# A batched transformer chain on one core: TensorE runs identity products into a bank before some of its waits, in the first three and last two batches

## The reference

```python
x = x + attn_a(layernorm(x), ...)   # latent attention: 16 heads, causal softmax over 512 keys
x = x + ffn(layernorm(x), ...)      # mixes each token with the one before it, then
x = x + attn_b(layernorm(x), ...)   #   sigmoid(xr @ W_r) * (relu(xk @ W_k)**2 @ W_v)
x = x + ffn(layernorm(x), ...)      # attn_b: queries and keys normalised per head, scale 8
```

## Time and profile before

| what | value |
|---|---|
| median of 3 runs | 1092.72 us (1090.68 to 1095.87) |
| profiled execution, its own time | 1093.79 us |
| its span, first to last instruction | 1092.0 us |
| mean granted TensorE clock | 0.951 |
| PE busy | 946.0 us (87%) |
| DVE busy | 877.3 us (80%) |
| ACT busy | 768.5 us (70%) |
| POOL busy | 281.8 us (26%) |

### The profile page before, as it was taken

The page is one execution under the profiler, slowest core; times in us unless marked ns, Lnnn a source line. Parts: engine busy times, 40 slices in busy tenths (PEclk is TensorE's granted clock), DMA queues, the critical chain, the costliest instruction groups (busy, mean ns, idle before and its releaser), DMA issues.

```text
span 1092.0 us, 37313 instructions
## 1 busy us (share of the span) xinstructions
PE 946.0 (87%) x15889; PEld 516.0 (47%) x15889; DVE 877.3 (80%) x2112; ACT 768.5 (70%) x1042; POOL 281.8 (26%) x264
## 2 busy tenths in 40 slices
PE   4687978888989899999999999998989899899694
PEld 1333444444544445454555545454545455455352
DVE  3977767889788898989899898989898888864633
ACT  2165557677767778787777778887777778788581
POOL 6111213223133131322223132223223232222212
PEclk8598889899999999999999999999999999999797
DMA  5243413455417062442617162543628170405220
GB/s 148 76 97 99 119 45 85 118 127 129 128 57 189 22 190 57 138 119 84 172 48 198 36 186 54 144 106 104 152 69 186 41 195 22 119 3 127 72 57 20
DMA packets 94342, 112.95 MB, mean 103 GB/s; under 512 B 15200, under 2 KB 81888, under 8 KB 94176
## 3 DMA queue, kind: packets, MB, share of 16 engines
q1 hardware_dynamic: 94176, 110.56, 38.6%
HBM read 55.22 MB, written 54.53 MB: 100 GB/s over the span
## 4 chain that ended last, share of the span: by engine, by line
PE 44%; DVE 31%; ACT 15%; issue 6%; POOL 1%; DMA 1%; SPq 0%; DVEq 0%; POOLq 0%; ACTq 0%
PE acc L729 14%; DVE rowmax L1081 11%; ACT prob L930 10%; PE pool L712 6%; PE pool L595 4%; PE pool L643 4%; PE pool L762 3%; DVE xn L1039 3%; PE pool L784 3%; PE pool L609 3%; DVE stats L1027 2%; PE pool L770 2%; PE pool L659 2%; DVE rest_k L1052 2%; PE pool L681 2%
## 5 line engine op out<-in xcount | busy, mean ns | idle before, releaser
L930 ACT ACTIVATE prob<-pool 128x1024 f32<-128x1024 f32 x576 | 565.3, 1030 | 136.3 <-PE pool L659 132.8
L1081 DVE TENSOR_REDUCE rowmax<-pool 128x2 f32<-128x1024 f32 (+7 forms) x480 | 357.2, 791 | 64.9 <-PE pool L659 62.2
L729 PE MATMUL acc<-prob,vals_a 128*32 128x512 f32 (+7 forms) x2048 | 167.7, 422 | 0.2 <-ACT prob L930 0.2
L729 PE MATMUL acc<-prob,vals_b 128*32 128x512 f32 (+7 forms) x2048 | 162.8, 418 | 1.5 <-DVE turned_b L1117 1.1
L643 PE MATMUL pool<-stack_ka,stack_qa 48*64 48x512 bf16 (+7 forms) x2048 | 117.0, 301 | 39.7 <-ACT prob L930 12.7
L712 PE MATMUL pool<-stack_qa,stack_ka 51*64 51x512 bf16 (+7 forms) x2048 | 113.3, 301 | 32.6 <-DVE rowmax L1081 18.4
L659 PE MATMUL pool<-mask_t,ident_b 64*64 64x128 bf16 (+1 forms) x2304 | 129.5, 215 | 0.0
L712 PE MATMUL pool<-stack_qb,stack_kb 48*64 48x512 bf16 (+7 forms) x2048 | 112.4, 295 | 17.1 <-ACT prob L930 8.3
L643 PEld LDWEIGHTS pool<-stack_ka,stack_qa 48*64 48x64 bf16 x2048 | 42.8, 108 | 131.8 <-issue 46.8
L1292 POOL TENSOR_TENSOR rstd<-mv,minus_half 128x4 f32<-128x4 f32 x64 | 65.4, 1022 | 146.1 <-DVE mv L1034 146.1
L712 PEld LDWEIGHTS pool<-stack_qa,stack_ka 51*64 51x64 bf16 x2048 | 42.8, 108 | 88.2 <-issue 26.3
(11 more groups left out here) (129 smaller groups left out, 1380.5 us busy)
## 6 DMA issues: line engine op xcount, KB each, us to landing
stack_qa<-scratch_qa SPq DMA_DIRECT2D x64, 192.0 KB, 4.9
stack_ka<-scratch_ka SPq DMA_DIRECT2D x64, 192.0 KB, 4.9
stack_kb<-scratch_kb SPq DMA_DIRECT2D x64, 192.0 KB, 3.9
stack_qb<-scratch_qb SPq DMA_DIRECT2D x64, 192.0 KB, 4.8
scratch_qa<-parts_q SPq DMA_DIRECT2D x16, 384.0 KB, 2.8
scratch_ka<-parts_k SPq DMA_DIRECT2D x16, 384.0 KB, 4.8
scratch_qb<-parts_q SPq DMA_DIRECT2D x16, 384.0 KB, 2.6
scratch_kb<-parts_k SPq DMA_DIRECT2D x16, 384.0 KB, 2.9
```

Of the source, the lines that this page charges most:

```text
L729: last = eng.matmul(acc[32 * j:32 * j + 32, BLK * blk:T], vals[a][:, blk, GROUP * g + j, :], prob[n % NPROB][:, k, at:at + T - BLK * blk], ...
L930: eng.activation(prob[n % NPROB][:, :, :], place["unit", n][0][:, :, :], ACT.Exp, scale=scale).then_inc(S["exped"], 1)
L1081: last = eng.tensor_reduce(to, of, axis=AX.X, op=ALU.max)
```

## The change

A row `"warm"` is added to each plan: one number for each of 22 places, named in `WARM_AT`. A new function `warm` issues so many products of the float32 identity with itself, 128 x 128 by 128 x 128, into the bank that the next product will overwrite. It is called between the wait for the bank and the wait for the input. No other number of the plans is changed, and no other engine's instructions are. A number counts once for each occurrence of its place in a batch (`max rows`, for one, occurs twice).

```diff
+WARM_AT = ("max", "max rows", "unit", "xnT1", "qa", "ka", "valsa", "ya", "xnT2", "k2", "r2", "v2", "xnT3", "qk", "qb", "kb",
+           "valsb", "wo", "xnT4", "k4", "r4", "v4")
...
     0: {
+        "warm": [0, 1, 0, 0, 0, 0, 5, 0, 1, 0, 0, 1, 3, 0, 0, 0, 2, 0, 0, 0, 0, 3],
...
     1: {
+        "warm": [0, 2, 0, 6, 1, 0, 0, 0, 0, 0, 0, 0, 0, 0, 0, 0, 0, 0, 2, 0, 0, 2],
...
     2: {
+        "warm": [0, 0, 0, 0, 0, 0, 0, 0, 0, 0, 0, 1, 0, 0, 0, 0, 0, 0, 1, 0, 0, 0],
...
     -2: {
+        "warm": [0, 0, 0, 0, 2, 2, 3, 0, 0, 0, 0, 0, 0, 0, 0, 0, 0, 0, 0, 0, 0, 0],
...
     -1: {
+        "warm": [0, 0, 0, 3, 0, 0, 0, 0, 0, 4, 0, 1, 5, 0, 0, 0, 0, 7, 4, 6, 2, 0],
...
+            def warm(self, ps, at, b):
+
+                plan = PLANS.get(b, PLANS.get(b - B, PLANS[None]))
+                for _ in range(plan["warm"][WARM_AT.index(at)]):
+                    self.eng.matmul(ps[:, 0:P], ident[:, :], ident[:, :], start=True, stop=True)
...
                 ps, freed = place["xnT" + n, b]
                 q.wait_free(freed)
+                self.warm(ps, "xnT" + n, b)
                 q.wait_ge(S["xn" + n], b + 1)
```

More of the change, by code:

```diff
@@ L35 @@
     None: {
+        "warm": [0, 0, 0, 0, 0, 0, 0, 0, 0, 0, 0, 0, 0, 0, 0, 0, 0, 0, 0, 0, 0, 0],
         "load": [-137],
@@ L617, in project @@
                     q.wait_free(freed)
+                    self.warm(ps, n + "a", b)
                     q.wait_ge(S["xnT1"], b + 1)
@@ L634, in row_maxima @@
                     q.wait_free(freed)
+                    self.warm(ps[:, 0, :], "max", b)
                     pieces = sum(max_pieces(*unit, NB), [])
@@ L666, in max_rows @@
                 q.wait_free(freed)
+                self.warm(ps, "max rows", b)
                 q.wait_ge(S["mpart2"], 2 * b + g + 1)
@@ L677, in values @@
                 q.wait_free(freed)
+                self.warm(ps, "vals" + a, b)
                 q.wait_ge(S["xnT" + n], b + 1)
@@ L699, in attend @@
                         q.wait_free(freed)
+                        self.warm(ps[:, 0, :], "unit", b)
                         q.wait_ge(S[f"stacked_q{a}{g}"], 32 * (b + 1))
@@ L739, in normalise @@
                     q.wait_free(freed)
+                    self.warm(ps, "ya", b)
                     q.wait_ge(S["outT_a"], GROUPS * b + g + 1)
@@ L754, in feed_forward @@
                 q.wait_free(freed)
+                self.warm(ps, "k" + n, b)
                 q.wait_ge(S["xk" + n], b + 1)
@@ L759, in feed_forward @@
                 q.wait_free(freed)
+                self.warm(ps, "r" + n, b)
                 q.wait_ge(S["xr" + n], b + 1)
@@ L767, in feed_forward @@
                 q.wait_free(freed)
+                self.warm(ps, "v" + n, b)
                 q.wait_ge(S["act" + n], b + 1)
@@ L780, in project_qk @@
                     q.wait_free(freed)
+                    self.warm(ps, "qk", b)
                     q.wait_ge(S["xnT3"], b + 1)
@@ L799, in turn_qk @@
                     q.wait_free(freed)
+                    self.warm(ps, n + "b", b)
                     q.wait_ge(S["qk"], 2 * (b + 1))
@@ L810, in output_sum @@
                 q.wait_free(freed)
+                self.warm(ps, "wo", b)
                 q.wait_ge(S["yT"], b + 1)
```

## The result

| | before | with the change |
|---|---|---|
| median | 1094.0 us (8 runs, 1090.68 to 1095.87) | 1098.18 us (8 runs, 1096.33 to 1101.66) |
| ratio to before | | 1.0053, 95% interval 1.0034 to 1.0072 |
| span of the profiled execution | 1092.0 us | 1096.3 us |

The account below looks back on a forecast made before the run. No engine was taken to bound the whole; they hand the path to one another. Start +2.8, middle +2.0 and end -0.7 gave +4.1 us, on the median 1096.8 us, range 1086.0 to 1102.0.

Parts of the forecast that it names:

- A: Start, batches 0 and 1: products delay reductions and transposes, the clock gives part back; +2.8 us, bounds -0.4 to 5.7.
- The price of one: One identity product on TensorE, priced from the values' rows: 0.275 us warm, 0.575 us cold.
- so they remain: Cold stretches from 103.4 and 1025.0 us begin after waits in which no product stands, so they stay.
- B: Middle: products straight on the chain cost their time, 26 others nothing; +2.0 us, bounds 2.0 and 9.2.
- The seven on the chain: Middle products where the chain runs through TensorE without idle time: 7 x 0.275 = 1.9 us.
- I count them at nothing, since these engines cover TensorE there: 26 middle products where the chain runs on VectorE or ScalarE: no cost, or 7.2 us if that cover is gone.
- C: End: transposes cold, `k` ends where it does now, `v` takes 1.10 for 1.67; -0.7 us, bounds -2.0 to +2.6.
- TensorE pays everywhere: Slower rival: the 26 middle products held to be covered reach the path; 1104.0 us, chance 0.20.
- Clock restored: Faster rival: products or their shift keep TensorE warm where it was cold; 1085.6 us, chance 0.17.
- The 54 us: Whole kernel's loss to the clock gate by the skill's formula, 0.049 x 1092; the prediction argued against such a sum.
- The signs: Expected after: VectorE idle near 36 to 39 us, transposes near 48, stack_ka near 63, cold stretches kept, end clock rising before 1084.
- signs of being wrong: Start reductions without idle time, clock rising before the six products ran, or a long cold stretch of batches 0, 1, 15 gone.

Follow-up runs that it names:

- rest: Against the kernel before, only the other 40 products, in batches 0, 1, 2, 14 and 15, none of the start's 14 or the end's 19: 1.0026, +2.8 us.
- waits2: Against the kernel before, 61 products, all in waits for an input, at 140, in batch 13, at 1014, in batch 15 and at the end: 0.9958, -4.6 us.
- waits: Against the kernel before, 61 products meant for waits alone, 12 of them misplaced in batch 14 where there is no wait: 1.0009.
- fill41: Against the kernel before, 8 products before the first turning of batch 0's maxima and one before the transposes of batch 1: 1.0010.
- start: Against the kernel before, only the 14 products of the start, in batches 0 and 1: 1.0052, +5.7 us.
- xnT6: Against the kernel before, only the six products before the transposes of batch 1: 1.0030, +3.3 us.
- valsa15: Against the kernel before, only fifteen products before the values of batch 0, in place of the change's five: 1.0030, +3.3 us.

## Why the prediction was right

The forecast was +4.1 us, 1096.8; it came out at 1098.2, +5.8. The direction and the main place of the loss, the start, were right. That the number came so near is in part luck: A came out twice as large as worked out, with more than half of it from two things that the sum didn't have. Step by step:

- **The price of one.** 0.575 cold and 0.275 warm were both too high. Cold the five took 2.30 us (34.08 to 36.38), 0.46 each, and the six 2.72 us (44.03 to 46.75); warm they cost 0.22 to 0.25. Identity products aren't cheaper than real ones: the cold row was a group of two, whose first instruction takes longer (single instructions of the values take 0.274 to 0.581 us in the trace before, those of the identity 0.275 to 0.583 in the one after), and of the warm rows the prediction took 1.10 and passed over `v`, with four in 0.91 us, 0.23 each.
- **A, the start, +2.8.** The part measures +5.7 (3.8 to 7.4). The mechanism of the direct delay was right, its size too large: the reductions were late by 0.8 us after the 1.1 of the first ones (1.7 us in the run of the five alone), against 2.6, since the products are cheaper and the clock rose before the values were done. The transposes were late by 2.5 (5.3 worked out), and the clock gave back some 2.4 (2.5 estimated), so the projection of keys ended only 0.5 us late (3.2 worked out). VectorE took the keys up 1.2 us late, against 2.8. That stack_ka was nevertheless used 2.5 us late, near the 2.8, is luck: 1.25 of it is the longer transfer. The other half of the loss is the cold stretch near 70 us, 2.8 to 3.1 us, whose coming and going I had held to be fixed. Neither was in the sum. The step that said of the cold stretches from 103.4 and 1025.0 "so they remain" doesn't hold in each execution: in the changed kernel's profile the first shrank from 13.6 to 3.2 us without a product in the wait ahead of it.
- **B, the middle, +2.0 with bounds 2.0 and 9.2.** The part measures +2.8 (1.3 to 4.4). The seven on the chain cost their time as told, 0.22 us each in place of 0.275. "I count them at nothing, since these engines cover TensorE there" holds for the 11 in batches 0 to 2 and fails for the 14 of batches 14 and 15, which cost 2.1 us (table of `rest`).
- **C, the end, -0.7.** As told in each step but the sixfold: the six took 2.77 us cold and didn't make `k` late. `v` took 1.16. Measured 0.0, with -0.7 inside the interval.
- **The rivals.** "TensorE pays everywhere" has half of the covered products right and half wrong, and fell short of 1104. "Clock restored" didn't come with the change, but filling only waits gave -4.6 us, so part of what it was priced at can be had. (It came to 1085.6, just below the range's lower end of 1086.0, though the text says that the range takes it in.) The 54 us by the formula of the Trainium skill ("TensorE: Matmul & The Clock Gate", section Terms) are far above what the runs reached. In the profile of `waits2` cold stretches of 3.4, 13.7 and 13.6 us are gone, and the kernel won 4.6. By the same formula of the Trainium skill these would be worth 15 us, an estimate from that page.
- **The signs.** VectorE's idle time at 37 us, the transposes near 47, stack_ka at 64 and the cold stretch at 1030 came as told. The clock at the end rose at 1088.1, which is 1083.2 less the 4.9 us of delay. One of the signs of being wrong, a long cold stretch gone, came in part: the one of 13.6 us from 103.4 was 3.2 us long.

## What to carry to other kernels

A product that only keeps TensorE's clock up is free in a wait for an input, if all of them together are shorter than that wait; read the wait from the trace, for each batch by itself, and leave some of it unused. Outside of a wait it costs its whole time, 0.22 to 0.25 us, where the work behind it is on the chain (48 ahead of `v`: +12.1 us), and nothing that could be seen for 11 of the change's 25 products off the chain. The busy share of TensorE doesn't tell which it will be, and neither does the chain of one trace for certain: 14 products that it called covered cost 2.1 us. Filled waits paid where TensorE's own work follows on the chain; in the one place where a transfer followed, nothing was won.

A single trace can't divide a gain of 1 to 3 us between places, since cold stretches of that weight come and go between executions of one kernel. It takes many executions, and a run with each part alone.

## What the runs showed of the hardware that was not expected

Where the cold stretches lie differs between executions by more than the program explains. A stretch of 3.4 to 6.8 us near 66 to 74 us stands in seven of the profiles, two of them (`waits` and `waits2`) without a product before it, and in none of the other seven; where it is 6.6 to 6.8 long it costs 2.7 to 3.1 us (in `waits` the starts on ScalarE go from 1.0 to 3.8 us late over it), and 1.5 us in `waits2` and `fill41`, where it is 3.4 long. Cold stretches go with the spread between runs of one kernel, 1089 to 1097 us: of the 100 executions of the kernel before that ran beside the experiments, the 12 with a mean clock of 0.946 to 0.949 took 1095.2 us on average, and the 21 with 0.955 or 0.956 took 1091.4.

The record of the clock can lack an entry. In the changed kernel the windows list the clock at the start as full,

```profile
26.70:36.00 9.30, 7.26 (x97) 4.68 (x98) 8.59 (x13) 0.00 (x0) 0.14 (x1) 1.00 0.36 67
```

while scores took 0.64 us each in it, as they did before at 0.50, and 0.41 later. The mean clock of 0.973 is too high for that reason; the durations of products tell the clock more safely. The profile of `start` lacks the same entry, and the twelve others list the clock as 0.50 from 17 to 20 us on.

TensorE waited 1.0 to 1.7 us for stack_ka of batch 1 in the changed kernel and in the runs `start`, `xnT6`, `fill41` and `valsa15`, and at most 0.4 us in all the others. All five have the cold stretch near 70 us, and of the nine others only `waits` and `waits2`: the wait and the stretch seem to belong together. In the same five, and in no other, SyncE took 0.6 to 1.3 us longer than usual over one of the issues of these transfers that follow (in the changed kernel 1.91 us for the last two, against 0.89). Which is cause and which effect, and why it comes with products at the start, was not found.
